# Last layer of a graph network stack: the attended product one period later, directly ahead of the scores

## The reference

```
        q = (x @ Wq + bq).reshape(b, n, H, HD)
        k = (x @ Wk + bk).reshape(b, n, H, HD)
        v = (x @ Wv + bv).reshape(b, n, H, HD)
        scores = jnp.einsum('bqhd,bkhd->bhqk', q, k) / jnp.sqrt(jnp.float32(HD))
        scores = scores + (1.0 - adj)[None, None, :, :] * -1000000000.0
        attn = jax.nn.softmax(scores, axis=-1)
        out = jnp.einsum('bhqk,bkhd->bqhd', attn, v).reshape(b, n, d)
        return out @ Wo + bo
    ...
    h = jnp.maximum(_layernorm(x, axis=-1), 0.0)
    x = x + _L3_gnn_ref(h, adj, L3_gnn_Wq, L3_gnn_bq, L3_gnn_Wk, L3_gnn_bk, L3_gnn_Wv, L3_gnn_bv, L3_gnn_Wo, L3_gnn_bo)
```

## Time and profile before

| | us |
|---|---|
| median of 3 runs | 734.18 (732.96 to 734.44) |
| the profiled execution | 734.51 |
| its span in the trace | 732.4 |
| TensorE busy | 706.3 |
| VectorE, ScalarE, GpSimd busy | 620.6, 565.5, 462.7 |

### The profile page before, as it was taken

How to read it: one execution, slowest core, us unless ns; L and a number is a source line. 1 busy time by engine, 2 the same in 40 slices (tenths; PEclk the granted TensorE clock), 3 DMA queues, 4 the chain that set the end, 5 groups by cost and what they waited for, 6 DMA issues and landing times.

```text
span 732.4 us, 22713 instructions
## 1 busy us (share of the span) xinstructions
PE 706.3 (96%) x6938; PEld 656.4 (90%) x6938; DVE 620.6 (85%) x2618; ACT 565.5 (77%) x1892; POOL 462.7 (63%) x585
## 2 busy tenths in 40 slices
PE   6999999999999999999998999999999999999996
PEld 5999999998788787889997999999999999999985
DVE  5898988886799898699997888888888888888875
ACT  3666565655688888976765999899989998999895
POOL 2455555455387688588885666766676666667662
PEclk9999999999999999999999999999999999999998
DMA  7322300000000000000000000000000000000001
GB/s 240 99 91 87 100 0 0 0 1 1 1 0 2 1 2 1 2 0 1 0 0 1 17 30 29 15 29 29 29 15 29 30 29 15 29 29 29 15 30 44
DMA packets 21701, 20.18 MB, mean 28 GB/s; under 512 B 2448, under 2 KB 21648, under 8 KB 21648
## 3 DMA queue, kind: packets, MB, share of 16 engines
q1 hardware_dynamic: 19456, 18.16, 7.6%
q10 hardware_dynamic: 2192, 1.44, 0.7%
HBM read 11.21 MB, written 8.39 MB: 27 GB/s over the span
## 4 chain that ended last, share of the span: by engine, by line
PE 87%; DVE 6%; issue 3%; ACT 2%; DMA 1%; POOL 0%; ACTq 0%; DVEq 0%
PE bank L395 43%; PE bank L1275 8%; PE bank L1261 5%; PE bank L385 5%; PE bank L166 5%; PE bank L1285 4%; PE bank L478 4%; PE bank L835 4%; PE bank L425 3%; PE bank L375 3%; DVE xs L853 1%; PE bank L459 1%; DVE att L1041 1%; PE bank L873 1%; DMA wk<-in_L_gnn_Wk_dram 1%
## 5 line engine op out<-in xcount | busy, mean ns | idle before, releaser
L1371 ACT ACTIVATE prob<-wide,small 128x128 f32<-128x128 f32 x504 | 195.9, 395 | 18.5 <-DVE small L1485 18.5
L1446 POOL TENSOR_TENSOR prob<-prob,small 128x512 f32<-128x512 f32 x127 | 132.3, 1042 | 108.4 <-DVE small L1499 106.9
L1485 DVE CUSTOM_DVE_ANT_0 wide<-bank,mbias 128x128 f32<-128x128 f32 x512 | 115.8, 283 | 10.2 <-PE bank L1261 10.1
L1371 ACT ACTIVATION_READ_ACCUMULATOR prob<-wide,small 128x1 f32 x504 | 96.8, 192 | 0.0
L155 POOL TENSOR_TENSOR rstd<-vare,mhalf 128x2 f32<-128x2 f32 x104 | 73.8, 710 | 20.7 <-DVE vare L144 20.4
L1391 ACT COPY probT<-bank 128x512 f32<-128x512 f32 x127 | 71.3, 588 | 9.3 <-PE bank L1275 8.6
L1275 PE MATMUL bank<-ident,prob 128*128 128x128 f32 x512 | 74.2, 278 | 2.7 <-POOL prob L1446 2.7
L634 POOL TENSOR_TENSOR rnorm<-norm,mhalf 128x2 f32<-128x2 f32 x32 | 22.3, 697 | 81.0 <-ACT relsq L575 81.0
L129 DVE BATCH_NORM_STATS2 stats<-xs 128x6 f32<-128x256 f32 (+1 forms) x176 | 65.7, 415 | 5.8 <-DMA xs<-in_x_dram 4.9
L239 POOL TENSOR_SCALAR xn<-xs,nmean,rstd 128x256 f32<-128x256 f32 x120 | 65.8, 559 | 5.5 <-POOL rstd L155 5.5
L1275 PEld LDWEIGHTS bank<-ident,prob 128*128 128x128 f32 x512 | 57.3, 141 | 9.9 <-issue 6.0
(11 more groups left out here) (163 smaller groups left out, 1881.5 us busy)
## 6 DMA issues: line engine op xcount, KB each, us to landing
out_dram<-xs SPq DMA_DIRECT2D x31, 256.0 KB, 2.1
xs<-in_x_dram SPq DMA_DIRECT2D x29, 256.0 KB, 2.7
xs<-in_x_dram ACTq DMA_DIRECT2D x1, 512.0 KB, 7.7
xs<-in_x_dram ACTq DMA_DIRECT2D x1, 256.0 KB, 4.1
wq<-in_L_gnn_Wq_dram SPq DMA_DIRECT2D x1, 256.0 KB, 3.7
wk<-in_L_gnn_Wk_dram ACTq DMA_DIRECT2D x1, 256.0 KB, 5.1
wv<-in_L_gnn_Wv_dram SPq DMA_DIRECT2D x1, 256.0 KB, 5.8
w<-in_L_gnn_W_dram SPq DMA_DIRECT2D x1, 256.0 KB, 7.4
```

Source lines behind the costliest of these rows:

```text
L1371: ins = nc.scalar.activation(prob[:, r, i, :], wide[:, r, i, :], ACT.Exp, bias=nmax[r][:, i:i + 1], scale=-1.0, accum_out=rsum[r][:, i:i + 1])
L1446: nc.gpsimd.tensor_tensor(prob[:, r, :, :], prob[:, r, :, :], rinv[r].unsqueeze(2).to_broadcast([128, QUAD, N]), ALU.mult).then_inc(prob_r ...
L1485: nc.vector.tensor_tensor_reduce(out=wide[:, r, i, :], in0=SS[r][:, i * N:(i + 1) * N], in1=mbias[:, :], scale=-1.0, scalar=3e38, op0=ALU. ...
```

## The change

All in the last layer; no arithmetic changes.

- TensorE: `attend(p-2)` now stands in period p, directly ahead of `scores(p)`, instead of `attend(p-1)` behind `project_k`. `project_q` stands directly behind the scores, then `project_o(p-2)`, then the turns of heads 2 and 3, then `project_k`. The loop's body is four periods, taken six times; three periods ahead and five behind are written out.
- Buffers: the turned weights of heads 0 and 1 go to `probT` for even pairs and to the two tiles `raw` for odd ones (free since the weights were prepared); the values use all four buffers `valb`.
- ScalarE: `exponentials(p-1, 3)` moves from the end of a period to the next period, behind `relu_high` and `copy_o(p-2)`; the turned heads 2 and 3 are copied behind the exponentials of head 1. Its loop has a body of two periods.
- GpSimd: the division of head 3 of the pair before moves behind the normalised input, `add_bias` between the divisions of heads 0 and 1.
- VectorE: moments first, then both low parts, then the masks; `copy_k` later, directly ahead of the last inverse and `copy_v`.

The diff, cut to its core:

```diff
--- before.py
+++ after.py
@@ -1227,6 +1227,9 @@
             half_y, sum_step = sem("l3_half_y"), sem("l3_sum_step")
             last_prob_ready = sem("l3_last_prob_ready")
             last_o, last_y = (SS[3], SS[2]), (SS[0], SS[1])
+            prob_turned = [[probT[:, r, :, :] for r in range(R)],
+                           [raw[r][:, :, :].rearrange("p c (i n) -> p (c i) n", n=N) for r in range(2)] +
+                           [probT[:, r, :, :] for r in range(2, R)]]
...
-                def attend(p, b):
+                def attend(p, v):
...
-                                                       valb[b][:, g, HD * h:HD * (h + 1)], probT[:, r, g * C + c, :],
+                                                       valb[v][:, g, HD * h:HD * (h + 1)], prob_turned[v % 2][r][:, g * C + c, :],
...
-                def period(p, b):
-                    if has(p, 0):
-                        scores(p)
-                    if has(p, 2, PAIRS - 1):
+                def period(p, v):
+                    if has(p, 2):
+                        attend(p - 2, (v + 2) % 4)
+                    scores(p)
+                    if has(p, 0, LAST):
+                        project_q(p + 1)
+                    if has(p, 2, LAST):
                         project_o(p - 2)
-                    if has(p, 1, PAIRS):
+                    if has(p, 1):
                         turn_prob(p - 1, 2)
                         turn_prob(p - 1, 3)
                     if isinstance(p, int) and p == LAST:
                         project_o(LAST - 2, TQ)
-                    if has(p, 0, PAIRS - 1):
-                        project_q(p + 1)
+                        attend(LAST - 1, (LAST - 1) % 4)
+                    if has(p, 0, LAST):
                         project_k(p + 1)
-                    if has(p, 1):
-                        attend(p - 1, 1 - b)
-                    if has(p, 0):
-                        turn_prob(p, 0)
-                    if has(p, 0, PAIRS - 1):
+                    turn_prob(p, 0)
+                    if has(p, 0, LAST):
                         project_v(p + 1)
-                    if has(p, 0, PAIRS - 2):
-                        turn(p + 2, b)
-                    if has(p, 0):
-                        turn_prob(p, 1)
+                    if has(p, 0, LAST - 1):
+                        turn(p + 2, v % 2)
+                    turn_prob(p, 1)
...
-                period(0, 0)
-                period(1, 1)
-                with pe.Fori(1, PAIRS // 2 - 1) as j:
-                    period(2 * j, 0)
-                    period(2 * j + 1, 1)
-                period(LAST - 1, 0)
-                period(LAST, 1)
+                for p in range(3):
+                    period(p, p)
+                with pe.Fori(0, PAIRS // 4 - 2) as j:
+                    for i in range(3, 7):
+                        period(4 * j + i, i % 4)
+                for p in range(LAST - 4, PAIRS):
+                    period(p, p % 4)
...
-                def copy_pT(p, r):
+                def copy_pT(p, r, b):
                     act.wait_ge(pt_done, R * p + r + 1)
-                    act.wait_ge(o_done, since(p))
-                    nc.scalar.copy(probT[:, r, :, :].rearrange("p i n -> p (i n)"), PT[r % 2][:, :]).then_inc(pt_ready, 1)
+                    act.wait_ge(o_done, since(p - 1 if r < 2 else p))
+                    nc.scalar.copy(prob_turned[b][r], PT[r % 2][:, :].rearrange("p (i n) -> p i n", n=N)).then_inc(pt_ready, 1)
 
                 def copy_o(p):
                     act.wait_ge(o_done, p + 1)
                     act.wait_ge(y_done, since(p))
                     nc.scalar.copy(oTs[0][:, :, :, :].rearrange("p g c n -> p (g c n)"), OT[:, :]).then_inc(o_high_ready, 1)
 
-                def period(p):
-                    if has(p, 1, PAIRS + 1):
-                        copy_pT(p - 1, 1)
-                    if has(p, 0, PAIRS - 1):
-                        relu_high(p + 1, TQ1 if isinstance(p, int) and p == 0 else TQ)
-                    if has(p, 0):
-                        exponentials(p, 0)
-                    if has(p, 1, PAIRS + 1):
-                        copy_pT(p - 1, 2)
-                        copy_pT(p - 1, 3)
-                    if has(p, 0):
-                        exponentials(p, 1)
-                    if has(p, 0):
-                        exponentials(p, 2)
-                    if has(p, 1, PAIRS + 1):
-                        copy_o(p - 1)
-                    if has(p, 0):
-                        copy_pT(p, 0)
-                        exponentials(p, 3)
-
-                period(0)
-                with act.Fori(1, PAIRS - 1) as p:
-                    period(p)
-                for r in range(1, R):
-                    copy_pT(LAST - 1, r)
+                def period(p, b):
+                    if has(p, 1):
+                        copy_pT(p - 1, 1, 1 - b)
+                    relu_high(p + 1, TQ1 if isinstance(p, int) and p == 0 else TQ)
+                    if has(p, 2):
+                        copy_o(p - 2)
+                    if has(p, 1):
+                        exponentials(p - 1, 3)
+                    exponentials(p, 0)
+                    exponentials(p, 1)
+                    if has(p, 1):
+                        copy_pT(p - 1, 2, 1 - b)
+                        copy_pT(p - 1, 3, 1 - b)
+                    exponentials(p, 2)
+                    copy_pT(p, 0, b)
+
+                for p in range(3):
+                    period(p, p % 2)
+                with act.Fori(1, PAIRS // 2 - 1) as j:
+                    period(2 * j + 1, 1)
+                    period(2 * j + 2, 0)
+                copy_pT(LAST - 1, 1, 0)
+                exponentials(LAST - 1, 3)
+                copy_o(LAST - 2)
                 exponentials(LAST, 0)
+                copy_pT(LAST - 1, 2, 0)
+                copy_pT(LAST - 1, 3, 0)
                 exponentials(LAST, 1)
                 copy_o(LAST - 1)
                 exponentials_last(2)
                 exponentials_last(3)
-                copy_pT(LAST, 1)
-                copy_pT(LAST, 2)
-                copy_pT(LAST, 3)
+                for r in range(1, R):
+                    copy_pT(LAST, r, 1)
...
                 for p in range(PAIRS):
-                    if has(p, 1):
-                        divide(p - 1, 3)
                     if p + 2 < PAIRS:
                         inverse_root(pool, p + 2, stats_ready, rstd_ready, p % 2)
                         pool.wait_ge(tr_done, p + 1)
                         centre(pool, p + 2, p % 2, rstd_ready, xn_ready)
                     if p == LAST - 1:
                         add_bias(LAST)
-                    if has(p, 0):
-                        divide(p, 0)
-                        divide(p, 1)
-                    if has(p, 0, LAST):
+                    if p > 0:
+                        divide(p - 1, 3)
+                    divide(p, 0)
+                    if p < LAST:
                         add_bias(p)
-                    if has(p, 0):
-                        divide(p, 2)
+                    divide(p, 1)
+                    divide(p, 2)
...
-                def copy_v(p, b):
+                def copy_v(p):
                     dve.wait_ge(v_done, p + 1)
-                    dve.wait_ge(o_done, since(p - 1))
-                    nc.vector.tensor_tensor(valb[b][:, :, 0:D], VV[:, :].rearrange("p (g d) -> p g d", g=2),
+                    dve.wait_ge(o_done, since(p - 3))
+                    nc.vector.tensor_tensor(valb[p % 4][:, :, 0:D], VV[:, :].rearrange("p (g d) -> p g d", g=2),
...
-                def last_periods():
+                def last_period():
                     inverse(LAST - 1, 3)
-                    for r in range(R):
+                    mask_max(LAST, 0)
+                    low_o(LAST - 2)
+                    for r in range(1, R):
                         mask_max(LAST, r)
                     inverse(LAST, 0)
                     update(LAST - 2, TQ)
@@ -1560,48 +1563,41 @@
                     update_half(0)
                     update_half(1)
 
-                def period(p, b):
-                    if has(p, 1, PAIRS + 1):
-                        inverse(p - 1, 3)
-                    if has(p, 0):
-                        mask_max(p, 0)
-                    if has(p, 1, PAIRS - 1):
-                        low_h(p + 1)
-                    if has(p, 2, PAIRS + 2):
-                        update(p - 2)
-                    if has(p, 0):
-                        mask_max(p, 1)
-                        inverse(p, 0)
-                        mask_max(p, 2)
-                    if has(p, 0, PAIRS - 1):
-                        copy_q(p + 1)
-                        copy_k(p + 1)
-                    if has(p, 0):
-                        inverse(p, 1)
-                        mask_max(p, 3)
-                    if has(p, 0, PAIRS - 3):
+                def period(p):
+                    norms = p + 3 < PAIRS
+                    if norms:
```

(42 more changed lines are left out.)

7 lines of the change are left out of this document (4 added, 3 removed).

## The result

The changed kernel takes 724.06 us (median of 4 runs, 723.97 to 724.73), the kernel before 734.13 on the same chip (4 runs, 732.96 to 734.44). The ratio is 0.9869, 95% interval 0.9855 to 0.9884. The forecast was 724.9, from 722.0 to 731.5.

What follows compares the result with a forecast made beforehand. TensorE, busy 706.3 of 732.4 us, was taken to set the pace. Periods -10.1, start +0.1 and tail +0.75 sum to -9.3 us: profiled run 725.2, median 724.9, range 722.0 to 731.5.

Steps and rivals of the forecast that it cites:

- The period: TensorE's steps between weight loads for one pair of graphs: 10.18 us against 10.51, 0.33 less, range 10.08 to 10.35.
- the prediction's signs: Weight loads: no wait over 0.25 before the scores, one of 0.2 before the attended product, none before head 0's turn.
- that unseen pair: Attended product directly to scores on TensorE, not in the earlier trace: hole taken as 0.20, between zero and 0.37.
- Two causes for one hole: The 0.33 us a period gained on TensorE is 0.20 for a change of shape and some 0.13 waiting for VectorE's copy.
- Rival B: Ahead of the scores: entry costs 0.37 whatever stands before it, 4.9 us less gain, 729.8 us; chance 0.17.
- Rival E: Attended product to scores: new change of shape nearly free, tail keeps its length, 721.5 us; chance 0.03.
- Rival C: Wait only moves: both new entries cost 0.37, or query waits 0.3 for relu and low half; 734.5 us, chance 0.10.
- Rival D: TensorE's longer loop body stalls at its seam, deciding from 1.9 us a seam; at 2.5 us, 737.4 us; chance 0.10.
- The others in time: ScalarE, VectorE and GpSimd keep up with TensorE mid-layer; ScalarE busy near 9.5 of 10.18 us, 0.9 idle.
- The ends: First two periods cost +0.1 us; the tail behind the last scores is 0.75 us longer than 18.8.

Runs made afterwards that it cites:

- Experiment 4: Kernel before, VectorE's value copy cut to one graph of the pair from pair 2 on, about 0.27 us shorter: 729.38 us, ratio 0.9942.
- Experiment 3: Changed kernel, attended product ahead of head 1's turn, head 3's turn behind key, VectorE's moments and ScalarE's head 2 copy earlier: 729.88 us, ratio 0.9948.
- experiments 1 to 4: First two: changed kernel, attended product ahead of head 1's turn, 734.21 us; same with head 3's turn behind key, 732.71 us. Other two have their own lines.
- experiment 7: Changed kernel with the attended output's copy ahead of relu on ScalarE and its low half first on VectorE: 752.53 us, ratio 1.0269.
- experiment 6: Changed kernel with an extra VectorE addition into an unused tile ahead of each value copy, 0.60 us: 726.97 us, ratio 0.9910.
- Experiment 9: Changed kernel with one more ScalarE copy into an unused tile at the end of each period, 0.63 us: 724.08 us.
- experiment 5: Kernel before with an extra VectorE addition into an unused tile ahead of each value copy, 0.60 us: 752.3 us, ratio 1.0253.
- Experiment 8: Changed kernel, last period only: ScalarE's exponentials and attended output ahead of turned head 1's copy, VectorE's low half ahead of the first mask: 723.22 us.

## Why the prediction was right

**The period.** Predicted 10.18, measured 10.20. The steps of the loads above: turn to attended product 0.64 (0.64 predicted), that to scores 1.01 (1.01), scores 1.10 (1.11), query 1.42 (1.43), output 1.42 (1.42), turns of heads 2 and 3 0.87 (0.86), key 1.44 (1.43), head 0 0.44 (0.43), value 1.45 (1.42), input 0.43 (0.43). That period is 10.22; others are 10.17 and 10.19. The new neighbours, attended product to scores, cost 0.20 of idle loads, as attended product to turn did before, and the step is 1.01 in both. The load ahead of the attended product has 0.17 idle, and the turn of head 0 none, as the prediction's signs have it. Bounding that unseen pair from both sides and taking the value of the nearest rows was right.

**Two causes for one hole.** The claim that the gain is part change of shape and part a wait for VectorE's copy holds; its split was off. Experiment 4 takes away only the wait: the step ahead of the scores shrinks by 0.16, the period by 0.14. Experiment 3 puts back only the shape: 0.155. The steps give 0.16 + 0.155 = 0.32 against the 0.31 measured. The prediction has 0.20 and some 0.13, though its own rows, 0.37 with 0.20 of shape in it, leave 0.17 for the wait. Why one change more costs 0.155 and not 0.20 stands in the earlier trace rows: the hole is 0.20, but the turn that begins behind a change of shape is through in 0.39 (615.88 to 616.27) instead of 0.43. The sum of the steps has that 0.04 in it, the split has not. By the rule alone of the Trainium skill (TensorEngine Tiling, Key Properties), one drain less, the estimate was 5.8 us at 0.20 each; 28 x 0.155 = 4.3 is what the runs give it.

**Rival B**, an entry into the scores that costs 0.37 whatever is ready, falls: experiments 1 to 4 enter them from a turn with 0.17 of idle loads, and the changed kernel from the attended product with 0.20. **Rival E**, a nearly free new change of shape and an end as long as before, falls by the same 0.20 and by the end's +0.71 below.

**Rival C**, the query waiting for relu and the low half, did not come, but its margin was as small as computed. Predicted 0.14; VectorE's low half and the query's load in period 2:

```profile
408.01 0.69 DVE L1504 SCALAR_TENSOR_TENSOR hTs<-bank,hTs 128x512 fp32r<-128x512 f32 x1 [0.29 <-ACT hTs L1368]
...
408.90 1.49 PEld L395 LDWEIGHTS bank<-hTs,wq 128*128 128x128 f32 x12
```

The low half ends at 408.70, and 0.05 later the query could load; it loads at 408.90, when the scores before it are through. That leaves 0.15. (The 0.05 is the time from the low half's end to the load in experiment 7, 622.35 to 622.41.) In experiment 7 the low half ends 2.04 after the scores' load (620.31), not 0.90: 1.14 later, of which 0.99 appears in the period, so 0.15 once more. Of the 0.6 in experiment 6 only a small part reaches this chain, and 0.05 comes out.

**Rival D**, the seam of a body of 1056 matmuls and loads, did not show, against the 1.9 us a seam from which it decides. The starts from pair 3 on are 10.17, 10.19, 10.22, 10.22 apart, over and over: across the seam (611.78 to 622.00) it is 10.22, inside the body (601.56 to 611.78) 10.22, and in the periods written out (683.16 to 693.38) also 10.22. The prediction applies to these loops the rule of the Trainium skill (Runtime: NRT & Kernel Launch, Instruction fetch mechanics) on branches out of the current two pages. No run here shows such a stall; whether the rule bears on TensorE's bodies, for which the same section gives an instruction memory of 2048, no run here tells.

**The others in time.** ScalarE was to be busy near 9.5 of 10.18, 93%; between 420 and 680 us it is busy for 234.9 of 260, 90%, or 9.2 a period. Experiment 9 shows 0.5 of its computed 0.9 to be free.

**The ends.** Predicted +0.1 for the first two periods: from the scores of pair 0 to those of pair 2 it is 18.44 after and 18.37 before, +0.07. Predicted +0.75 for the tail: from the last scores to the end of the span 19.54 after (722.7 - 703.16) and 18.83 before (732.4 - 713.57), +0.71. Both of these ends have a stretch at a lower granted clock. At the full clock the changed kernel has 18.43 (its repeat), and the old end 17.72 and 17.75 (experiments 4 and 5, which leave what lies behind the last scores as it was): +0.7 again. The mechanism is the one given, VectorE's inverse waiting for ScalarE's exponentials of the pair before. On VectorE at the end, the counterpart of the earlier trace rows:

```profile
704.42 0.18 DVE L1500 RECIPROCAL small<-small 128x4 f32<-128x4 f32 x1 [1.91 <-ACT prob L1374]
...
708.52 0.17 DVE L1500 RECIPROCAL small<-small 128x4 f32<-128x4 f32 x1
```

The first stands 1.26 after the scores, and the inverse behind the masks 5.36 after them, where it was 4.64 before. Experiment 8 gives back 0.65 of it: 17.78, at the full clock.

**Where the hit was partly luck.** From pair 2 to pair 31 the profile gives -9.55 us, predicted -10.12: a period of 10.20 instead of 10.18, 28 times, mainly the value projection's step of 1.45. Against it, the first scores begin 0.93 earlier (389.36, before 390.29), though nothing ahead of them was changed; over the profiles without the longer copy of experiments 5 and 6 this start lies anywhere from 389.31 to 390.29. The forecast did not have it. The spans' difference is -0.93 + 0.07 - 9.55 + 0.71 = -9.70; without that chance start it would be -8.77, against a forecast of -9.3. The medians lie 10.07 apart, since the changed kernel's median is an execution with the shorter end (last section), 0.67 below the profiled one.

## What to carry to other kernels

Where an engine is busy all the time, look at the steps between the starts of its products, not at its busy share: two products of the same kind with different steps show a hole. Then ask of a hole how much is a cost and how much a wait; a wait moves when its cause is moved (the step from the copy's start, 0.92, with TensorE full or empty, gave it away), a change of array shape stays. And when an order is put back to test one cause, look for the waits that the old order brings with it: twice here an order that was meant to restore one hole of 0.17 brought another 0.1 on a different engine, and the time alone would have proved the wrong theory.

## What the runs showed of the hardware

**A change of the array's shape** costs about the same here between all pairs met. From a turn into 128x32 or 32x128 the weight loads are idle for 0.17 us, out of 128x32, to 128x128 or straight to 32x128, for 0.20. Out of 32x128 the scores' matmuls show it (one lasts 0.27):

```profile
611.78 1.17 PE L1264 MATMUL bank<-kT,qT 32*128 32x128 f32 x32
```

The last starts at 612.68, and the next load is at 612.88, 0.20 later. Four changes a period against three differ by 0.155, since the next turn is shorter by 0.04.

**From the end of another engine's work to TensorE's load** the time depends on the place. It is 0.05 for the low half and the query (experiment 7, 622.35 to 622.41), and 0.23 for the value copy and the scores (experiment 5, 620.91 to 621.14, and in the earlier trace rows). The 0.18 more is not a change of shape as such: that query also changes the shape, behind the scores, and so does the last attended product, which in the repeat of the changed kernel is loaded 0.06 after ScalarE's last copy ends at 715.96:

```profile
716.02 0.11 PEld L1299 LDWEIGHTS bank<-raw,val 128*32 128x32 f32 x2 [0.92 <-ACT probT L1394]
```

So where TensorE has stood idle, in these two places for 1.11 and 0.92, the 0.20 of a change of shape does not show. The scores differ by their entry into 32x128 and by waiting on four semaphores, the query on one; which of the two makes the 0.18 is not tested.

**The end of the kernel has two lengths.** The output projection of pair 30, near the end, in the changed kernel's first profile and in the second:

```profile
712.00 2.64 PE L395 MATMUL bank<-wo,oTs 128*128 128x256 f32 x12 [0.47 <-DVE oTs L1509]
```

```profile
712.30 1.64 PE L395 MATMUL bank<-wo,oTs 128*128 128x256 f32 x12 [0.47 <-DVE oTs L1509]
```

The first has a mean granted clock of 0.998 over the span, the second 1.000. From 712.5 to 715.5 the granted clock is 0.50 in the first, the level of 1.2 GHz, and 1.00 in the second. What TensorE did before it hardly differs: from 705 to 711 it was busy for 3.86 of 6 us in the first and 3.97 in the second, with idle stretches of up to 1.29 in which it waited for GpSimd's divisions. So the clock falls there in some executions and not in others. From the last scores to the end it is 19.54 against 18.43, 1.1 us, more than experiment 8 wins. Of the changed kernel's eight timed executions the two with 0.998 took 724.73 and 724.68, the six with 1.000 from 723.93 to 724.11. All four of experiment 8 had 1.000, so its gain of 0.85 is one of like against like. A difference of one microsecond between single executions of this kernel says nothing.
